# Sliding attention with value products per head in a new order, and a third layer norm read from PSUM

## The reference

```
tok:  q,k,v = x@q_w+q_b, ...                      # 8 heads of 16
      q kept for the 50 tokens with the largest |q|^2 per head, else 0
      attn_out = softmax(q k^T / 4) v @ o_w + o_b
      h1 = layernorm(x + attn_out)                # first norm
      h2 = layernorm(h1 + relu(h1@f1_w+f1_b)@f2_w+f2_b)   # second norm
      h  = maxpool2(relu(conv3(h2 + attn_out)))   # 250 -> 125 tokens
attn: n3 = layernorm(h)                           # third norm
      q,k,v = n3 @ W_qkv + b ; softmax over keys at distance <= 32, per head
      h = h + (probs v) @ W_proj + b_proj
ffn:  h = h + layernorm(h) on 128 features        # the table columns it adds lie outside
```

## Time and profile before

| | |
|---|---|
| median of 3 runs | 592.61 us (591.25 to 595.72) |
| profiled execution | 590.11 us, its span 588.3 us |
| granted TensorE clock, mean | 0.944 |
| busy share | PE 86%, DVE 71%, ACT 63%, POOL 46% |
| feed-forward steps, about 184 to 390 us | a step takes 12.85 us |
| sliding attention, about 397 to 562 us | a slot takes 4.87 us |
| output, from 567.5 us | transfers only after 572 us |

### The profile page before, as it was taken

How to read it: one execution, slowest core, us unless ns; L and a number is a source line. 1 busy time by engine, 2 the same in 40 slices (tenths; PEclk the granted TensorE clock), 3 DMA queues, 4 the chain that set the end, 5 groups by cost and what they waited for, 6 DMA issues and landing times.

```text
span 588.3 us, 13845 instructions
## 1 busy us (share of the span) xinstructions
PE 505.1 (86%) x4554; PEld 352.7 (60%) x4554; DVE 417.8 (71%) x1694; ACT 371.5 (63%) x1115; POOL 272.4 (46%) x218
## 2 busy tenths in 40 slices
PE   6997999999986999999989999976888888888830
PEld 4686666676654666666666666644666666666510
DVE  3798578888854688878888887635777777777750
ACT  5975588889874344454444445436788888888740
POOL 2760677878865766666665666421111111111030
PEclk9999599999996999999999999986999999999965
DMA  4441122222220000000000000000000000000013
GB/s 153 141 138 37 43 50 59 62 58 59 63 70 29 26 21 31 20 19 20 17 19 20 30 4 1 2 0 0 2 1 3 2 2 2 2 2 2 2 38 103
DMA packets 21914, 19.87 MB, mean 34 GB/s; under 512 B 14180, under 2 KB 18436, under 8 KB 21716
## 3 DMA queue, kind: packets, MB, share of 16 engines
q1 hardware_dynamic: 21268, 18.28, 11.0%
q10 hardware_dynamic: 576, 0.71, 0.4%
HBM read 16.81 MB, written 2.18 MB: 32 GB/s over the span
## 4 chain that ended last, share of the span: by engine, by line
PE 25%; ACT 19%; DVE 9%; POOL 7%; issue 6%; DVEq 0%; ACTq 0%; POOLq 0%
ACT wprobs L977 10%; PE bank L829 6%; DVE n L1112 5%; PE quad L784 4%; POOL hb L1060 3%; POOL hb L1058 3%; PE quad L852 3%; PE bank L909 3%; ACT wprobsT L1003 2%; PE quad L776 2%; ACT oF L995 2%; PE bank L858 2%; ACT woT L1010 2%; ACT ao L942 1%; PE quad L807 1%
## 5 line engine op out<-in xcount | busy, mean ns | idle before, releaser
L476 POOL TENSOR_SCALAR put<-keyb,c 100x1000 f32<-100x1000 bf16 x32 | 89.1, 2784 | 43.6 <-DMA keyb<-key_scratch 27.8
L1078 POOL TENSOR_TENSOR kbd<-wkT,c 128x250 f32<-128x250 f32 x32 | 19.3, 602 | 134.1 <-ACT wkT L985 134.1
L977 ACT ACTIVATE wprobs<-quad,wmax 125x125 f32<-125x125 f32 x256 | 73.1, 384 | 1.8 <-DVE wmax L1166 0.7
L1166 DVE CUSTOM_DVE_ANT_0 quad<-quad,c 125x125 f32<-125x125 f32 x256 | 65.7, 320 | 11.6 <-PE quad L852 8.0
L609 ACT ACTIVATE probs<-quad,negmax 100x250 f32<-100x250 f32 x128 | 58.4, 468 | 19.8 <-DVE negmax L561 18.6
L784 PE MATMUL quad<-h1T,w 128*128 128x500 f32 x128 | 60.7, 598 | 0.4 <-ACT hid L948 0.3
L807 PE MATMUL quad<-w,hid 128*125 128x128 f32 x512 | 59.0, 273 | 0.1
L807 PEld LDWEIGHTS quad<-w,hid 128*125 128x125 f32 x512 | 57.4, 188 | 0.9 <-issue 0.5
L948 ACT ACTIVATE hid<-quad,vec_cols 128x500 f32<-128x500 f32 x64 | 43.0, 676 | 9.8 <-PE quad L784 8.1
L491 PE MATMUL bank<-c,probs 100*125 100x100 f32 x256 | 46.8, 309 | 2.2 <-ACT probs L609 1.4
L491 PEld LDWEIGHTS bank<-c,probs 100*125 100x125 f32 x256 | 35.5, 202 | 19.9 <-issue 12.2
(11 more groups left out here) (138 smaller groups left out, 1227.1 us busy)
## 6 DMA issues: line engine op xcount, KB each, us to landing
keyb<-key_scratch SPq DMA_DIRECT2D x64, 97.7 KB
xa<-xT SPq DMA_DIRECT2D x8, 500.0 KB, 3.6
xt<-xtok SPq DMA_DIRECT2D x16, 250.0 KB
out<-o_all SPq DMA_DIRECT2D x4, 500.0 KB
w<-weights SPq DMA_DIRECT2D x1, 1024.0 KB, 7.3
vec_rows<-rows SPq DMA_DIRECT2D x1, 448.0 KB, 5.4
c<-consts ACTq DMA_DIRECT2D x1, 428.5 KB, 5.9
w<-weights ACTq DMA_DIRECT2D x1, 192.0 KB, 4.4
```

Source lines behind the costliest of these rows:

```text
L476: nc.gpsimd.tensor_scalar(put[u % 3][:, :, :], keyb[p][:, :, :], c[0:ROWS, CONST["sidx"]], None, ALU.is_equal).then_inc(put_done, 1)
L977: ins = nc.scalar.activation(probs[p][:, j, :], s_of(j), ACT.Exp, bias=negmax[p][:, j:j + 1], scale=-1.0)
L1166: ins = nc.vector.tensor_tensor_reduce(s_of(j), s_of(j), c[0:LH, CONST["band"]], 1.0, OFF, ALU.add, ALU.min, negmax[p][:, j:j + 1])
```

## The change

In the third norm, VectorE's two normalising instructions read `h_bank` in PSUM, where they read `h0`. The copy to `h0` stays, for the statistics and for GpSimd.

In the sliding attention the value products swap operands: `probsT` of a head is loaded and 17 columns of `vo` (16 values and one of ones) stream, so the output is token-major. The copy `oT` and its two transposes go. The reciprocal and `otok` read the products' bank in the slot after. The projection goes to another bank (`x_bank`) and stands just before the value products; the transpose of `otok` stands behind the transposes of heads 4 to 7. `oF` moves from ScalarE to VectorE, and the copy of `probsT` for heads 4 to 7 on ScalarE moves up by one pair of exponentials.

```
@@ TensorE, window
-                    nc.tensor.transpose(y_of, otok[:, :], ident[0:LH, 0:LH]).then_inc(oF_ready, 1)
...
                 if within(u, 2, B + 2):
-                    pe.wait_ge(oF_done, u - 1)
-                    nc.tensor.matmul(y_proj, oF[:, :], w[:, WEIGHT["wp"]], start=True, stop=True).then_inc(proj_ready, 1)
+                    pe.wait_ge(otok_done, u - 1)
+                    nc.tensor.transpose(y_of, otok[:, :], ident[0:LH, 0:LH]).then_inc(oF_ready, 1)
...
+                if within(u, 2, B + 2):
+                    pe.wait_ge(oF_done, u - 1)
+                    pe.wait_ge(v_done, min(u + 1, B))
+                    wait(pe, z_done, u - 2)
+                    nc.tensor.matmul(x_proj, oF[:, :], w[:, WEIGHT["wp"]], start=True, stop=True).then_inc(proj_ready, 1)
+
                 if within(u, 1, B + 1):
-                    wait(pe, z_done, u - 1)
+                    wait(pe, oF_done, u - 1)
...
                     for j in range(H):
-                        ins = nc.tensor.matmul(y_bank[CW * (j % 4):CW * (j % 4) + CW, LH * (j // 4):LH * (j // 4) + LH],
-                                               vo[pm][:, j, :], probsT[pm][:, j, :], start=True, stop=True)
+                        ins = nc.tensor.matmul(y_o[:, j, :], probsT[pm][:, j, :], vo[pm][:, j, :], start=True, stop=True)
                     ins.then_inc(pv_ready, 1)
-
-                if within(u, 1, B + 1):
-                    pe.wait_ge(oT_done, u)
-                    for i in range(2):
-                        ins = nc.tensor.transpose(y_a[:, 128 * i:128 * i + 128], oT[:, LH * i:LH * i + LH], ident)
-                    ins.then_inc(otok_ready, 1)
@@ ScalarE, window
-                    nc.scalar.activation(oF[:, :], y_of, ACT.Identity, bias=col("wv_b")).then_inc(oF_done, 1)
                 if within(u, 0, B):
                     wait(act, pT0_ready, u - 1)
                     exponents(0)
-                    exponents(1)
                 if within(u, 1, B + 1):
                     act.wait_ge(pT1_ready, u)
...
                 if within(u, 0, B):
+                    exponents(1)
                     exponents(2)
                     exponents(3)
-                    nc.scalar.activation(oT[:, :], y_bank[:, 0:2 * LH], ACT.Copy).then_inc(oT_done, 1)
@@ VectorE, ffn
-                    normalise(2, n3, h0, 2, t - 1)
+                    normalise(2, n3, tok(h_bank, 2), 2, t - 1)
@@ VectorE, window
+                if within(u, 2, B + 2):
+                    dve.wait_ge(pv_ready, u - 1)
+                    wait(dve, otok_done, u - 2)
+                    nc.vector.reciprocal(rinv[:, :], y_o[:, :, HD]).then_inc(rinv_done, 1)
...
+                    dve.wait_ge(oF_ready, u - 1)
+                    wait(dve, proj_ready, u - 2)
+                    nc.vector.tensor_scalar(oF[:, :], y_of, col("wv_b"), None, ALU.add).then_inc(oF_done, 1)
```

More of the change, by code:

```diff
@@ L38 @@
 CW = 2 * HD
+VW = HD + 1
 ROWS = 2 * KTOP
@@ L698, in ffn_and_window @@
         kbd = pair("kbd_", [128, 2, LH])
-        vo = pair("vo_", [LH, H, CW])
+        vo = pair("vo_", [LH, H, VW])
         negmax = pair("wmax_", [LH, H])
@@ L702, in ffn_and_window @@
         probsT = pair("wprobsT_", [LH, H, LH])
-        oT = sb("woT", [128, 2 * LH])
         rinv = sb("wrinv", [LH, H])
@@ L727, in ffn_and_window @@
         x_k, x_q, x_v = x_bank[:, 0:LH], x_bank[:, 128:128 + LH], x_bank[0:LH, 256:256 + D]
-        y_a, y_of, y_proj = y_bank[0:LH, 256:512], y_bank[:, 0:LH], y_bank[0:LH, 128:128 + D]
+        x_proj = x_bank[0:LH, 384:384 + D]
+        y_o, y_of = y_bank[0:LH, 0:H * VW].rearrange("p (h f) -> p h f", h=H), y_bank[:, 256:256 + LH]
         def s_of(head):
@@ L984, in window @@
                         act.wait_ge(v_ready, u + 1)
+                    wait(act, z_done, u - 2)
                     nc.scalar.activation(kT[:, :], x_k, ACT.Identity, bias=col("wk_b")).then_inc(kT_done, 1)
@@ L989, in window @@
                     act.wait_ge(v_ready, u + 1)
+                    wait(act, z_done, u - 2)
                     wait(act, pv_ready, u - 1)
                     nc.scalar.activation(vo[p][:, :, 0:HD], x_v.rearrange("p (h f) -> p h f", h=H), ACT.Copy).then_inc(v_done, 1)
-                if within(u, 2, B + 2):
-                    act.wait_ge(oF_ready, u - 1)
-                    wait(act, proj_ready, u - 2)
-                    nc.scalar.activation(oF[:, :], y_of, ACT.Identity, bias=col("wv_b")).then_inc(oF_done, 1)
                 if within(u, 0, B):
@@ L1159, in window, with mask_and_min @@
                 um2, _, _ = shift(h, p, -2)
[L1161 to L1167, removed]
-                if within(u, 0, B):
-                    mask_and_max(0)
-                    mask_and_max(1)
+                def mask_and_min(lo, hi):
+                    for j in range(lo, hi):
+                        ins = nc.vector.tensor_tensor_reduce(s_of(j), s_of(j), c[0:LH, CONST["band"]], 1.0, OFF, ALU.add, ALU.min,
+                                                             negmax[p][:, j:j + 1])
+                        if j % 2:
+                            ins.then_inc(min_done, 1)
+                if within(u, 2, B + 2):
+                    dve.wait_ge(pv_ready, u - 1)
+                    wait(dve, otok_done, u - 2)
+                    nc.vector.reciprocal(rinv[:, :], y_o[:, :, HD]).then_inc(rinv_done, 1)
+                    dve.wait_ge(rinv_done, u - 1)
+                    wait(dve, oF_ready, u - 2)
+                    nc.vector.tensor_tensor(otok[:, :].rearrange("p (h f) -> p h f", h=H), y_o[:, :, 0:HD],
+                                            rinv[:, :].unsqueeze(2).to_broadcast([LH, H, HD]), ALU.mult).then_inc(otok_done, 1)
+                if within(u, 0, B):
+                    dve.wait_ge(scores, u + 1)
+                    mask_and_min(0, 4)
+                if within(u, 2, B + 2):
+                    dve.wait_ge(oF_ready, u - 1)
+                    wait(dve, proj_ready, u - 2)
+                    nc.vector.tensor_scalar(oF[:, :], y_of, col("wv_b"), None, ALU.add).then_inc(oF_done, 1)
+                if within(u, 0, B):
+                    mask_and_min(4, 8)
                 if within(u, 2, B + 2):
@@ L1175, in window @@
                         dve.wait_ge(h0b_done, NP)
[L1176 to L1182, removed]
+                    nc.vector.tensor_tensor(z_all[:, um2:um2 + 1, :], x_proj.unsqueeze(1), z_all[:, um2:um2 + 1, :], ALU.add).then_inc(z_done, 1)
                 if within(u, 0, B):
@@ L1186, in window @@
                     nc.vector.tensor_copy(probsT[p][:, 0:4, :].rearrange("p h l -> p (h l)"), t_bank[0][0:LH, 0:4 * LH]).then_inc(pT0_done, 1)
[L1187 to L1195, removed]
+                if within(u, 2, B + 2):
+                    dve.wait_ge(z_done, u - 1)
+                    nc.vector.bn_stats(zst[:, um2:um2 + 1, :].rearrange("p a b -> p (a b)"), z_all[:, um2:um2 + 1, :].rearrange("p a b -> p (a b)")).then_inc(stat, 1)
             def spread(lo, hi, count):
```

9 lines of the change are left out of this document (2 added, 7 removed).

## The result

The changed kernel takes 627.61 us, median of 4 runs (624.45 to 633.03); the kernel before took 591.93 us in the 4 runs beside them. The ratio is 1.060, 95% interval 1.051 to 1.070: slower, and by more than twice the forecast 2.1%. The profiled execution took 629.05 us with a span of 627.2 us, against 590.11 and 588.3 before, so 38.9 us have to be found.

A forecast was written before the change was run, and what follows sets the result against it. Short waits bound the feed-forward steps, a loop through TensorE, VectorE and ScalarE the sliding attention. From 590.1 us, −11.0, +2.0, +3.5, +19.6 and −1.8 gave 602.4; with runs' median 2.5 higher, 605 us, range 588 to 640.

The forecast's parts named there:

- The entry: Start of the sliding attention: TensorE at 1.2 GHz in slots 1 and 2, +2.0 and +3.5 us.
- rival A: Sliding attention: low clock comes back; a third of 28 slots +26, 631 us, all +79, 684 us; chance 0.28.
- Part 1: Feed-forward steps: third norm from PSUM takes 0.70 us beside GpSimd, TensorE's wait goes, −11.0 us.
- Part 2: Sliding attention: value products with `probsT` loaded take 16 loads at 0.107 us, 1.71 us a slot.
- Rival B: Value products: narrow loads cost what the 32-column loads cost, products 0.65 us, slot 4.51, kernel 570 us; chance 0.12.
- Part 3: Sliding attention's new order: slot of 5.57 us, 0.70 longer than 4.87, +19.6 us over 28 slots.
- Slot 1: First slot of the sliding attention: value products at low clock take 3.4 us, +2.0 us in all.
- slot 2: Second slot of the sliding attention: still at low clock, 8.4 us in all, +3.5 us.
- The end: After the last slots: clip 31 dealt with after the output factors, output transfers start earlier, −1.8 us.
- The sum: Whole kernel: 590.1 us with −11.0, +2.0, +3.5, +19.6 and −1.8 gives 602.4 us; 605 us predicted.
- C: Feed-forward steps: the norm from PSUM does not free VectorE, the 11.0 us stay, 616 us; chance 0.07.
- D: Sliding attention: loop lengthens half as much, 9.8 us not 19.6, slot 2 at full clock, 592 us; chance 0.12.

The follow-up runs named there:

- e1: The kernel before with only the third norm read from PSUM; 580.00 us, ratio 0.980.
- e4: The changed kernel with value products writing 32 columns a head instead of 17; 617.83 us, ratio 1.046.
- e9: e7 with `oF` on VectorE after the sixth mask, VectorE's copy ahead of the projection's sum and value products ahead of the projection; 561.40 us, ratio 0.949.
- e3: The changed kernel with ScalarE's copy of heads 4 to 7 back behind the second pair of exponentials; 605.42 us, ratio 1.0225.
- e6: The changed kernel with the value products moved ahead of the transposes of heads 0 to 3, into TensorE's wait; 641.68 us, ratio 1.083.
- e5: The changed kernel with four unread 128-column products a slot in the wait before the transposes of heads 0 to 3; 603.35 us, ratio 1.020.
- e7: e1 with the old value products in a new order like the changed kernel's, the copy of heads 4 to 7 in its old place; 571.80 us, ratio 0.965.

## Why the prediction was wrong

The step that failed is the clock after "The entry": the term for the low clock in slots 3 to 30 was put at nothing, and it measured 23.6 us. The forecast took the clock as low in slots 1 and 2 and full in the 28 after them, and left the rest to rival A. Rival A is what happened. It had a chance of 0.28, and a price that holds: "each low slot costs 8.4 − 5.57 = 2.8 us" is 8.38 − 5.63 = 2.75 as measured, "a third of 28 slots: +26, 631 us" stands beside 23.6 and 627.61 us. The argument that weighed against it, that the denser half of the slot may lift the clock again, did come true: the clock rises again and again, and falls again as often. It was no reason for a term of nothing. A mechanism that lifts and one that lowers give a mixture, and a mixture should have been the forecast; how much of each, no row of the kernel before could tell, and that rival A's third was so near is luck.

Point by point:
- **Part 1** was right: pair 0.73 us (forecast 0.70), steps 11.89 (12.0), 12.6 us gained up to the scores of clip 1 (11.0 booked). e1 measures it alone: 11.4 up to there, and 10.9 in the medians. By the Trainium skill (SBUF — State Buffer, "Who interferes with whom") a VectorE instruction with at most one input in SBUF, outside the two-port modes, does not contend with GpSimd; the trace agrees for this pair, which reads PSUM: 0.73 us beside a running GpSimd instruction against 1.69.
- **Part 2** was right: 1.82 us for sixteen loads (1.71), 0.109 us a load (0.107). Rival B falls. e4 shows that the loads are the bound. The 0.65 us that the prediction takes for products "as now" stands in none of its rows; the trace of e9 has 0.60.
- **Part 3** was right at full clock: 5.63 us against 5.57. The copy's 0.47 is 0.48 by e3. VectorE's cover held; e6 shows what its failure costs, masks 0.76 us late and the slot longer by all of it. TensorE's own work was put too low, 4.3 us where it is busy 4.61; that didn't lengthen a slot at full clock.
- **Slot 1** +1.35 (forecast +2.0), **slot 2** +3.5 (+3.5).
- **The end**, forecast −1.8, came at +1.7. The order's part is right at the clock of before (−1.9 in e5 up to the transfers). At low clock the waits of clip 30 for TensorE, which stand ahead of the factors in VectorE's queue, make it +0.8. So 2.7 us of the miss here are the low clock again, and 0.9 came behind the start of the transfers, where the prediction had no change.
- **The sum** without the low clock in slots 3 to 30 would be 590.1 − 12.6 + 4.9 + 21.3 + 1.7 = 605.4 us, where the forecast's sum for this execution is 602.4 (its 605 adds 2.5 for the median). The end measured 3.5 us more than forecast and slots 3 to 30 at full clock 1.7 more, part 1 and the entry 2.2 less, 3.0 in all. With 23.6 us more it is 629.0.

Rivals C and D fall by e1 and by the slot of 5.63 us.

## What to carry to other kernels

- In a product with few streamed columns the loads set the time, and turning the product round so that the long operand is loaded multiplies it: here 0.40 us for sixteen loads of 32 columns, 1.82 for sixteen of 125, and 0.60 against 1.85 us from the first load to the next instruction.
- A walk along one period's waits can be right to 1% and the kernel's time still miss by 4%, if the period holds for one level of the clock only. When a change thins what TensorE does in a period of several us, work out the period at both levels and forecast a mixture of them, above all when the entry to the stage already runs low.
- The price of a stretch holds for the clock at which it was read: the same end of the kernel took 10.97 us at a granted clock of 0.81 and 13.67 at 0.50.
- Before a step is moved to follow a late result, list all that its engine has queued behind that result: in e6 it was five VectorE instructions ahead of the masks.

## What was not expected of the hardware

Added work made the kernel faster: 0.88 us of unread products a slot (an estimate, eight loads at 0.11 us) brought 627.61 to 603.35 us, and 0.44 us of them in e3's order brought 605.42 to 589.99, with the slots at full clock unchanged. TensorE's records show the same busy share, 0.88 to 0.90, in loops that keep 2.4 GHz (e1, e7) and in one that does not (e3). The Trainium skill (TensorE: Matmul & The Clock Gate, "A second HAM failure mode: psum-queue depth-cycling") tells of a kernel whose clock swings because TensorE pauses briefly between groups of products. The swing is in the trace here, between 1.00 and 0.50; that pauses alone bring it is not, since e1 pauses for as large a share and keeps 1.00. What it is in the narrow products (their few columns, or that they wait for their loads) was not separated: e4, the run for it, was inconclusive.
